# A Perceiver block in one kernel: down-projection chunks loaded into the places of their ternary weights, and an opening split by k-tiles and halves

## The reference

```
x = x + xattn(layernorm(x), ctx)      # q = x Wq', k, v = ctx Wkv'; 16 heads of 64; causal softmax; Wout
x = x + bitmlp(layernorm(x))          # below
x = x + moe(layernorm(x))             # rms norm, top 2 of 8 experts (1024 -> 512 -> 1024) and a shared expert

bitmlp: y = bitlinear(x, w_gate, norm_gate); gate, up = split(y)       # 1024 -> 2 x 2816
        h = silu(gate) * up;  return bitlinear(h, w_down, norm_down)   # 2816 -> 1024
bitlinear(x, w, norm): xn = rms_norm(x) * norm
        xq = round(xn * 127 / max|xn|) * max|xn| / 127                 # one scale per row
        wq = clip(round(w / mean|w|), -1, 1) * mean|w|                 # ternary, one scale per matrix
        return xq @ wq.T
```

## Time and profile before

| | |
|---|---|
| runs, us | 676.99, 677.55, 678.81 |
| profiled execution, us | 677.46 |
| its span, us | 675.9 |
| TensorE busy | 634.3 us, 94% |
| VectorE busy | 490.8 us, 73% |
| ScalarE busy | 411.0 us, 61% |
| GpSimd busy | 145.0 us, 21% |
| moved by DMA | 179.02 MB, mean 265 GB/s |

### The profile page before, as it was taken

One profiled execution on the slowest core, in us unless ns is written; L12 is line 12 of the kernel. 1 busy time (PEld: TensorE's weight loads), 2 busy tenths in 40 slices (PEclk: granted clock), 3 DMA queues, 4 the chain that ended last, 5 costly groups with the idle time before them and its releaser, 6 DMA issues.

```text
span 675.9 us, 9662 instructions
## 1 busy us (share of the span) xinstructions
PE 634.3 (94%) x3275; PEld 476.4 (70%) x3289; DVE 490.8 (73%) x790; ACT 411.0 (61%) x531; POOL 145.0 (21%) x140
## 2 busy tenths in 40 slices
PE   4899999998999999839999999999999999999996
PEld 3778888886885444325467878787878778787875
DVE  5778888879686898688898376729181983654887
ACT  3778888789647998672674275436171771625730
POOL 1363446406000344319500400000000000000042
PEclk9999999999999999959999999999999999999999
DMA  8867776764166878808987639938385697392947
GB/s 340 359 259 291 288 288 234 316 268 176 46 271 269 332 297 362 340 16 305 411 328 263 247 140 380 390 119 332 135 297 198 223 378 330 125 360 69 390 146 277
DMA packets 30969, 179.02 MB, mean 265 GB/s; under 512 B 3808, under 2 KB 3808, under 8 KB 14688
## 3 DMA queue, kind: packets, MB, share of 16 engines
q1 hardware_dynamic: 25920, 161.39, 61.6%
q0 software_dynamic: 5024, 17.30, 6.8%
HBM read 155.62 MB, written 23.07 MB: 264 GB/s over the span
## 4 chain that ended last, share of the span: by engine, by line
PE 56%; DVE 15%; ACT 15%; issue 5%; DMA 5%; POOL 1%; DVEq 1%; SPq 0%; POOLq 0%; ACTq 0%
PE BK L295 12%; PE BK L296 11%; PE BK L301 11%; PE BK L289 9%; ACT PR L1224 4%; ACT RA L1197 3%; PE BK L1700 3%; PE BK L1600 2%; DVE WL L951 2%; PE BK L1823 2%; PE BK L1585 1%; DMA GB<-rows,SLOT 1%; DMA RA<-wbit 1%; DMA rows<-YS 1%; DVE BH L838 1%
## 5 line engine op out<-in xcount | busy, mean ns | idle before, releaser
L295 PE MATMUL BK<-WH,ETH 128*128 128x512 f32 x272 | 107.6, 396 | 1.4 <-ACT ETH L1445 1.3
L296 PE MATMUL BK<-WL,ETH 128*128 128x512 f32 x272 | 106.1, 390 | 0.0
L951 DVE TENSOR_TENSOR WL<-RA,WH 128x2048 fp32r<-128x2048 f32 x40 | 89.4, 2286 | 9.6 <-ACT WH L1412 9.5
L1412 ACT ACTIVATE WH<-RA 128x2048 fp32r<-128x2048 f32 x40 | 73.7, 1922 | 2.3 <-PE BK L1700 2.3
L301 PE MATMUL BK<-WH,ETL 128*128 128x512 f32 x272 | 67.4, 390 | 0.0
L1471 ACT ACTIVATE HTH<-BK 128x256 fp32r<-128x256 f32 x30 | 10.7, 383 | 88.6 <-PE BK L1823 88.5
L295 PEld LDWEIGHTS BK<-WH,ETH 128*128 128x128 f32 x272 | 51.0, 188 | 16.6 <-DVE WL L951 3.8
L649 POOL DMA_INDIRECT GA<-rows,SLOT x4 | 4.9, 1230 | 265.1 <-DVE WL L951 264.1
L301 PEld LDWEIGHTS BK<-WH,ETL 128*128 128x128 f32 x272 | 51.0, 188 | 10.6
L296 PEld LDWEIGHTS BK<-WL,ETH 128*128 128x128 f32 x272 | 51.1, 188 | 10.1
L617 POOL TENSOR_TENSOR HB<-HB,ND (+2 forms) x28 | 31.1, 1128 | 111.4 <-DVE BH L838 110.6
(11 more groups left out here) (260 smaller groups left out, 1409.8 us busy)
## 6 DMA issues: line engine op xcount, KB each, us to landing
RA<-wbit SPq DMA_DIRECT2D x53, 1024.0 KB, 6.4
RA<-wmoe SPq DMA_DIRECT2D x40, 1024.0 KB, 6.7
RC<-wmoe SPq DMA_DIRECT2D x20, 1024.0 KB, 7.5
rows<-ZERO POOLq DMA_DIRECT2D x34, 256.0 KB, 12.4
XG<-rows SPq DMA_DIRECT2D x15, 512.0 KB, 7.2
RD<-wbit SPq DMA_DIRECT2D x7, 1024.0 KB, 5.5
rows<-YS SPq DMA_DIRECT2D x14, 512.0 KB, 6.6
RA<-wqk SPq DMA_DIRECT2D x8, 640.0 KB, 7.4
```

What stands on the lines that cost most here:

```text
L295: e.matmul(dst, sh, mh, start=first and i == 0, stop=False)
L296: e.matmul(dst, sh, ml, start=False, stop=False)
L951: e.tensor_tensor(WL[m][:, q * RAW:q * RAW + RAW], RC[j][:, :], WH[m][:, q * RAW:q * RAW + RAW].bitcast(f32), ALU.subtract)\
L1412: e.activation(WH[m][:, q * RAW:q * RAW + RAW], RC[2 * m + q][:, :], ACT.Copy)\
```

## The change: what it does, and the diff

The opening. The context's two k-tiles are loaded apart, and the value weights' second k-tile comes between the row tiles of x. The value projection is ordered by k-tile and half: for the first k-tile, all four token tiles high by high, then low by high, then high by low, for one half and then the other; then the second k-tile, with the other half first. It uses eight banks. The low part of the second k-tile's weights moves from VectorE to GpSimd. ScalarE takes the root after the first value tile and normalises row tiles 1 and 3. All four row tiles are transposed after the values. The first query and key weights come into RX[1], and ScalarE makes their high part. The key projection goes before the query projection. The first split copies of keys and queries go ahead of sums on ScalarE and VectorE.

The down weights. Chunks 0, 2 and 8 are loaded to where they and their neighbour end (0 and 2 in TD1, 8 in TD2) and rounded and clamped there; 1 and 9 use RD, 3 uses RD2, 4 to 7 RB as before, 10 uses RB[0]. Loads of 0, 1, 2, 3 and 8 wait for no clamp. Three roundings (8, 9, 10) move behind the first two hidden tiles on ScalarE, their clamps behind the second scale on VectorE. The root part of `hidden_scale` becomes `hidden_root`, ahead of the last maxima. The sign of chunk 4 moves behind the last SiLU. The first expert load moves behind the next three.

```diff
-VB = (6, 7, 0, 1)
+VB = ((6, 7, 0, 1), (2, 3, 4, 5))
-DORD = (0, 1, 2, 3, 8, 9, 6, 7, 10)
+DORD = (0, 2, 1, 3, 6, 7, 8, 9, 10)
+RORD = (0, 2, 1, 3, 4, 5, 6, 7, 8, 9, 10)
...
+        RIN = {i: nc.alloc_sbuf_tensor_at(f"RIN{i}", [P, RAW], f32, offset=T.manual_sbuf_range[0] + at)
+               for i, T, at in ((0, TD1, 0), (2, TD1, 8192), (8, TD2, 0))}
+        def down_raw(i):
+            return RIN[i] if i in RIN else {1: RD, 3: RD2, 4: RB[0], 5: RB[1], 6: RB[2], 7: RB[3], 9: RD, 10: RB[0]}[i]
...
         def _(e):
-            e.dma_start(CTX[:, :, :], ctxT).then_inc(s("ctx_in"), 16)
+            e.dma_start(CTX[:, 0, :], ctxT[:, 0, :]).then_inc(s("ctx_in"), 16)
             e.dma_start(RA[0][:, 0:DM], wv[:, 0:DM]).then_inc(s("wv_in"), 16)
-            e.dma_start(RA[0][:, DM:2 * DM], wv[:, DM:2 * DM]).then_inc(in_a[0], 16)
+            e.dma_start(CTX[:, 1, :], ctxT[:, 1, :]).then_inc(s("ctx_in2"), 16)
             for t in range(NT):
+                if t == 2:
+                    e.dma_start(RA[0][:, DM:2 * DM], wv[:, DM:2 * DM]).then_inc(in_a[0], 16)
                 e.dma_start(XRES[:, t, :], x[t * P:t * P + P, :]).then_inc(s(f"x_in{t}"), 16)
+            e.dma_start(RX[1][:, 0:STRIP], wqk[0]).then_inc(in_x[1], 16)
...
-            qk_load(0)
             for n in range(4):
                 sum_load(1 + n, 4 + n, None)
-            for j in range(2):
-                e.dma_start(RX[j][:, :], wbit[8 + j]).then_inc(in_x[j], 16)
+            e.dma_start(RX[0][:, :], wbit[8]).then_inc(in_x[0], 16)
             qk_load(1)
+            e.dma_start(RX[1][:, :], wbit[9]).then_inc(in_x[1], 16)
...
-            down_load(0, 0, None)
+            down_load(1, "raw_d")
...
                 bit_load(n, 8 + n, "tern_a", 1 + n)
+            down_load(0, in_x[0])
             e.wait_ge(s("zq"), NT)
-            down_load(1, 1, None)
+            down_load(2, in_x[1])
+            down_load(3, "raw_e")
+            down_load(8, "raw_8")
             for n in range(4):
                 bit_load(n, 12 + n, "tern", 5 + n)
-            for n in range(2):
+            for n in range(4):
                 bit_load(n, 16 + n, "tern", 9 + n)
-            down_load(2, 0, 1)
-            for n in range(2, 4):
-                bit_load(n, 16 + n, "tern", 9 + n)
-            down_load(3, 1, 2)
...
-            down_load(8, 0, 3)
...
-            down_load(9, 1, 4)
             for n in range(2):
                 bit_load(n, 2 * GC + 4 + n, "tern", 17 + n)
-            down_load(10, 0, 5)
+            e.wait_ge(s("ternd"), DORD.index(1) + 1)
+            down_load(9, "raw_d")
+            bit_load(0, 2 * GC + 10, "tern_a", 5)
...
-                for j in range(6):
+                for j in (1, 2, 3, 0, 4, 5) if first else range(6):
...
+            for n, q in enumerate((1, 0)):
+                cs = slice(q * 512, q * 512 + 512)
+                e.wait_ge(s("wv_hi"), n + 3)
+                e.wait_ge(s("wv_lo"), 2)
+                e.tensor_tensor(WVL[:, 1, cs], RA[0][:, DM + q * 512:DM + q * 512 + 512], WVH[:, 1, cs].bitcast(f32),
+                                ALU.subtract).then_inc((s("wv_lp"), free_a[0])[n], 1)
+            for q, at in enumerate((slice(0, WQA * P), slice(WQA * P, STRIP))):
+                if q == 0:
+                    e.wait_ge(s("xn"), 2)
+                e.wait_ge(s("wq_hi"), q + 1)
...
+                e.tensor_tensor(lo, RX[1][:, at], hi.bitcast(f32), ALU.subtract).then_inc((s("wq_a"), free_a[0])[q], 1)
...
             absum(2, slice(5, 6), 16)
+            k_split(0)
             absum(4, slice(7, 8), 16)
-            k_split(0)
+            q_split(0)
             absum_x(1, 9)
-            q_split(0)
...
-            down_clamp(9, RD16)
+            down_clamp(3)
             last_block(2)
             last_maximum(0)
             last_maximum(1)
             last_block(3)
+            hidden_root(0, 2)
             last_maximum(2)
             last_maximum(3)
             hidden_scale(0, 2)
...
-            down_clamp(6, RB16[2])
-            down_clamp(7, RB16[3])
-            down_clamp(10, RD16A)
+            down_clamp(6)
+            down_clamp(7)
+            hidden_root(2, 2)
             for n in range(4, 8):
                 last_maximum(n)
             hidden_scale(2, 2)
+            down_clamp(8)
+            down_clamp(9)
+            down_clamp(10)
             hidden_integers(2)
...
-            for n in range(4):
+            v_evac(0)
+            root(e, col(2), col(3))
+            for n in range(1, 4):
                 v_evac(n)
-            root(e, col(2), col(3))
+            row_norm(1)
             v_evac(4)
             v_evac(5)
+            row_norm(3)
             xt_evac(0)
             xt_evac(1)
             v_evac(6)
+            xt_evac(2)
             v_evac(7)
-            xt_evac(2)
             xt_evac(3)
...
+            k_split(0)
             absum(1, slice(4, 5), 16)
             absum(3, slice(6, 7), 16)
+            q_split(0)
             e.wait_ge(in_x[0], 16)
             e.activation(RX[0][:, :], RX[0][:, :], ACT.Abs, accum_out=ACCW[:, 8:9]).then_inc(sum_x[0], 1)
-            k_split(0)
-            q_split(0)
...
             group(3)
-            rounded_down(RD[:, :], s("raw_d"), 1)
             group(4)
-            rounded_down(RD2[:, :], s("raw_e"), 1)
+            rounded_down(0)
             group(5)
-            rounded_down(RD[:, :], s("raw_d"), 2)
             group(6)
-            rounded_down(RD2[:, :], s("raw_e"), 2)
+            rounded_down(2)
             group(7)
-            rounded_down(RD[:, :], s("raw_d"), 3)
             gate_block(8, 0)
             gate_block(8, 1)
-            rounded_down(RD2[:, :], s("raw_e"), 3)
+            rounded_down(1)
             gate_block(8, 2)
             gate_block(8, 3)
-            rounded_down(RB[0][:, :], in_b[0], 6)
+            rounded_down(3)
             for n, (c, t) in enumerate(TAIL):
...
-                if n == 1:
-                    rounded_down(RB[1][:, :], in_b[1], 6)
-                elif n == 3:
-                    sign_down(4, 0, 7)
-                elif n == 4:
-                    rounded_down(RB[2][:, :], in_b[2], 5)
-                elif n == 6:
-                    rounded_down(RB[3][:, :], in_b[3], 5)
+                if n in (1, 3, 4, 5):
+                    rounded_down({1: 4, 3: 5, 4: 6, 5: 7}[n])
+            sign_down(4, 0, 5)
...
             hidden_t(0)
-            rounded_down(RD[:, :], s("raw_d"), 4)
-            sign_down(5, 1, 8)
+            sign_down(5, 1, 6)
             hidden_t(1)
+            rounded_down(8)
+            rounded_down(9)
+            rounded_down(10)
             hidden_t(2)
...
+            def values_first(q):
+                cs = slice(q * 512, q * 512 + 512)
+                for n, (A, B) in enumerate(((CTH, WVH), (CTL, WVH), (CTH, WVL))):
+                    e.wait_ge(*((s("wv_hi"), q + 1), (s("ct_lo"), 1), (s("wv_lo"), q + 1))[n])
+                    for t in range(NT):
+                        e.matmul(bank[VB[q][t]], A[:, 0, t * P:t * P + P], B[:, 0, cs], start=n == 0, stop=False)
...
+            values_first(0)
+            values_first(1)
+            e.wait_ge(s("ct_lo"), 2)
+            e.wait_ge(s("wv_lp"), 1)
+            values_rest(1)
+            e.wait_ge(free_a[0], 1)
+            values_rest(0)
             e.wait_ge(s("const"), 15)
-            x_rows(0)
-            x_rows(1)
-            values(6)
-            values(7)
-            x_rows(2)
-            x_rows(3)
-            e.wait_ge(s("v_ev"), 2 * NT)
-            e.wait_ge(s("xt_lo"), 2 * NT)
+            e.wait_ge(s("v_ev"), NT)
+            for t in range(NT):
+                x_rows(t)
+            e.wait_ge(s("v_ev"), 6)
...
             e.wait_ge(s("tern_a"), 6)
-            e.wait_ge(s("ternd"), 8)
+            e.wait_ge(s("ternd"), 6)
             down_group(0, 1)
             down_group(1, 1)
             e.wait_ge(s("ternd"), 9)
```

More of the change, by code:

```diff
@@ L574, in zero_rows, with w_split @@
                 e.dma_start(src.rearrange("a (u v) -> (a u) v", u=2), ZERO[:, :]).then_inc(s("zero"), 16)
-            def w_split(c, first, second=False):
+            def w_split(c, second=False):
                 for q, at in enumerate((slice(0, WQA * P), slice(WQA * P, STRIP))):
                     if q == 0:
-                        e.wait_ge(in_a[0], c * 16 + 32)
-                        if not first and not second:
+                        e.wait_ge(in_a[0], c * 16 + 16)
+                        if not second:
                             e.wait_ge(s("pn"), c * 2 - 2)
-                    if not first:
-                        e.wait_ge(s(("k_pe", "q_pe")[q]), c)
+                    e.wait_ge(s(("wq_pe" if second else "k_pe", "q_pe")[q]), c)
                     hi, lo = (T[:, :, :].rearrange("p a b -> p (a b)")[:, at] for T in (WQH, WQL))
@@ L667, in _, with context_lo @@
-            e.wait_ge(s("ln"), 1)
-            for t in range(NT):
+            def context_lo(m):
```

(56 more changed lines are left out.)

140 lines of the change are left out of this document (66 added, 74 removed).

## The result

The kernel after takes 669.5 us, the median of four runs (669.24 to 670.50); the kernel before took 677.9 beside it (four runs, 676.99 to 678.81). The ratio is 0.9877, with a 95% interval of 0.9855 to 0.9898: 8.4 us faster. The forecast was 664.0, the range 661.0 to 669.0. The sign was right, the gain was over-estimated by 5.5 us, and the measured time lies 0.5 us outside the range. The profiled execution took 670.50 us, 6.96 less than the one of before.

A forecast was written before the change was run, and what follows sets the result against it. TensorE's pace was taken to bound all long stages, with two large waits, at the start and at the hidden rows. 677.46 - 2.3 (opening) - 11.4 (tail) = 663.8, forecast as 664.0 us, range 661.0 to 669.0.

The forecast's parts named there:

- The opening: Start to first exponentials: exponentials at 37.3 instead of 39.6, worth 2.3 us, with bounds of 0.5 to 3.4.
- The tail: Gate products' end to hidden tile 2: tile 2 starts at 308.4 instead of 319.73, a gain of 11.4 us.
- the walk along VectorE's queue: Late gate stage: VectorE's work timed piece by piece, so TensorE transposes at 287.1, 1.5 us after the gate products end.
- a rival of the down stage: Down stage: VectorE becomes the bound, 2 to 6 us late, clamps taking 1.13 instead of 0.68; 666 to 670, chance 0.10.
- May arrive a microsecond late … Nothing.: Gate stage: three down loads in one 7.5 us burst delay a gate load a microsecond; TensorE 6.9 us ahead, no cost.
- The clock in the tail: Rival: after the gate products TensorE's clock falls, losing 2.2 to 3.5 us; 666.0 to 667.3, chance 0.2.
- a row of the kernel before: Opening, 25.4 to 29.2: TensorE did only transposes and its clock stayed at 1.00, so transposes seem to hold it.
- The rule that it weighed against that row: Opening: transposes don't engage the full clock, so it would fall there, costing 2 to 3.5 us; chance 0.05.
- No new wait at hidden tile 2: Down stage: late clamps and VectorE's integers for tile 2 are ready before TensorE needs them, by 0.5 us.
- The sign of chunk 4: Tail: ScalarE runs it after the last SiLU, 286.3 to 288.2, delaying its first copy of transposed rows.
- The slower rival: Down stage: the clock falls and stays low through all 176 down products, 35 us in sum; 699, chance 0.02.

The follow-up runs named there:

- e12: e9 with the opening of the kernel before, so only the down weights' part of the change plus e9's edits; 667.52 us.
- e13: e9 timed again, on the same chip as e12; 666.22 us.
- e1: Kernel after with the loads of down chunks 2, 3 and 8 taken out of their burst and spread behind gate loads; 669.21 us.
- e6: Kernel after with 20 extra matmuls, results unread, filling TensorE's wait ahead of the hidden transposes; 668.2 us.
- e5: Kernel after with down chunk 1's clamp and half the last chunk pair's maxima moved behind tile 0's integers on VectorE; 667.16 us.
- e2: Kernel after with only down chunk 8's load moved out of the burst, behind the gate loads; 669.12 us.
- e3: Kernel before with only the opening's part of the change; 677.09 us.
- e9: Kernel after with the edits of e1 and e5 and 9 of the extra matmuls of e6; 665.9 us.
- e4: Kernel before with only the down weights' part of the change; 669.87 us.
- e8: Kernel after with ten extra matmuls, results unread, among the opening's row-tile transposes; 669.45 us.
- e7: Kernel after with one weight sum of ScalarE and one of VectorE moved from before the exponentials into the first pair; 680.18 us.
- e11: e7 with the third pair's query and key weight load going first on the sync queue; 679.86 us.

## Why the prediction was right and wrong

**By its steps, the sum.** 13.7 us were forecast. The opening is worth 1.5 instead of 2.3 in the two profiles (1.3 in e12 and e13). From the gate products' end to hidden tile 2 the forecast had 308.4 - 285.65 = 22.75 us (34.08 before); it took 311.58 - 284.13 = 27.45. These 4.7 us divide into 2.6 for VectorE's list (the gap of e1, 4.1, less 1.5), 1.3 for the late load (5.4 less 4.1) and 0.7 from the transposes to the second down run (9.09 for 8.4), where the clock is: with it held, e6 took 8.20. The tail gained 6.65 us instead of 11.4. Of the 8.4 us between the medians that leaves 1.8 for the opening, inside what its traces show.

**The step that failed: the walk along VectorE's queue.** "VectorE takes tail blocks 0 and 1 by 276.6, a maximum and a clamp by 278.4, blocks 2 and 3 by 280.9" led to a gap of 1.5 us. Without any late load (e1) it is 4.1. The mechanism was right, the root ahead of the late maxima and nobody waiting for a load; the size was off. Taking the gate products' 1.8 us earlier end in e1 into account, its blocks 0 and 1 should have been done by 274.8 and were by 277.3, 2.5 late, and everything behind them (root 3.1, maxima 0.7, chain 1.2) took what was forecast. So the walk was wrong where it starts: its 276.6 is 1.3 us behind TensorE's second tail product, as if VectorE had nothing left to do ahead of these blocks. The kernel before had shown both the backlog and the price of a pair of gate clamps, in rows that the prediction did not read:

```profile
270.24 2.65 DVE L810 TENSOR_SCALAR TX<-RA 128x2048 bf16<-128x2048 int16 x2
...
275.11 2.27 DVE L843 TENSOR_REDUCE AMAX<-HB 128x4 f32<-128x2048 f32 x1
```

Those maxima (`pair_max(3)`) ended at 277.38, after the 276.6 of the forecast, and in the new order four blocks and a clamp stand between them and the end of blocks 0 and 1, 4.0 us in e1. So an end at 276.6 needed the maxima by 272.6, 13.0 us ahead of the gate products' end. They ended 8.3 us ahead of it before, and 10.4 in e1: 2.6 us short, the whole of the missing gap.

Part of the backlog is the price of the clamps. The pair ahead of these maxima took 2.99 us, where pairs elsewhere take 1.28. Over the whole kernel after, the same instruction ranges from 0.68 to 1.76 us (shortest, median, longest in ns):

```profile
L835 DVE TENSOR_SCALAR TG<-RA x12: 676/688/1760, 182.4 to 260.3; 128x2048 bf16<-128x2048 int16 x12
L835 DVE TENSOR_SCALAR TX<-RA x6: 676/1144/1759, 242.1 to 268.8; 128x2048 bf16<-128x2048 int16 x6
```

The long ones stand beside GpSimd's products with norm_down, three of which run from 265.79 to 269.97, across the pair at 267.53. Two pairs and GpSimd's work at that time:

```profile
254.57 3.01 DVE L835 TENSOR_SCALAR TG<-RA 128x2048 bf16<-128x2048 int16 x2
259.68 1.28 DVE L835 TENSOR_SCALAR TG<-RA 128x2048 bf16<-128x2048 int16 x2
```

```profile
251.62 5.42 POOL L625 TENSOR_TENSOR HB<-HB,ND  x4 [7.45 <-DVE BH L862]
264.56 5.41 POOL L625 TENSOR_TENSOR HB<-HB,ND  x4 [7.52 <-DVE BH L862]
```

All four pairs that run while GpSimd multiplies took 2.36 to 3.01 us, all three that run while it rests 1.28 or 1.29. The Trainium skill (SBUF — State Buffer, Who interferes with whom) says that VectorE and GpSimd share one pair of ports, which a VectorE instruction in a two-port mode also takes (a tensor_scalar such as the clamp can run in one), and that whoever has it blocks the other for a whole instruction; the trace agrees, with a clamp of 0.68 stretched to 1.76. No run here took GpSimd's work away, so that GpSimd is the cause is argued from the rows only. The prediction did name such clamps (1.13 for 0.68), but as a rival of the down stage. They mattered 20 us and more earlier, where VectorE has no idle time. That each piece in its list counts there is shown by e5.

**"May arrive a microsecond late … Nothing."** The load was late by 4.58 us of ScalarE's time, and the slack of one group of products had to carry it through a stretch in which VectorE fills nearly its whole time; 0.9 to 1.3 us of the gap are shown by e1 and e2. Costing the burst against TensorE's need was the error: VectorE was the engine without slack.

**The clock in the tail.** The forecast took it to hold, and gave its fall 0.2 and 2.2 to 3.5 us. It fell in the kernel after and in each execution with an unfilled gap (3.55 us and more), and cost 0.7 to 0.9 us (e6), since the transposes at half speed partly hide behind the integers that they wait for anyway. No run had an unfilled gap of 1.5 us, so whether the clock would have held there, and the fall comes from the failed step, is not shown.

**The opening.** The first matmul (6.29 for 7.0), the first low part (22.32 for 22.3) and the last (27.65 for 27.4) came as forecast or sooner. The scores came at 35.18 for 34.4, the exponentials at 38.13 for 37.3: ScalarE's chain of copy, sum, value copy and table load was right in its parts, but starts with a query copy that ends at 34.4 and not at 33.5. Most of that is the clock, which the prediction held by a row of the kernel before. Where it held, the scores came at 34.1 to 34.7 and the exponentials at 37.0 to 37.6 (e2, e3, e5, e9, e13), as forecast. The rule that it weighed against that row, that the full clock doesn't engage for PE-mode transposes (the Trainium skill, TensorE: Matmul & The Clock Gate, Part 4: PE-mode transpose), is borne out by the kernel after, e1 and e6, and not by five others with the same opening (e2, e3, e5, e9, e13), in which the clock stayed at 1.00 through 20 to 28. With the opening of before it held in the kernel before and e12 and fell in e4 (0.50 from 30 to 32). The fall costs some 0.6 us at the exponentials and at the gate products' end (e8), less than the timed runs can tell. So against the 39.60 of the profile before, the 2.3 us were there at the exponentials in these executions (2.0 to 2.6). That as much reaches the end of the program is shown by no timed run.

**What held.** No new wait at hidden tile 2: VectorE's integers ended at 310.46, 1.1 us ahead of TensorE (a margin of 0.5 was forecast), so the three late roundings and clamps are free. From the second down run to hidden tile 2 it took 12.95 us for 12.9. The sign of chunk 4 ended at 288.03 as forecast, but held nobody, since the integers came later still. The slower rival (clock low through all down products) did not come: the clock was back at 293.9.

## What to carry to other kernels

When a wait is closed, the next bound is the engine that feeds it: walk that engine's list with the durations that its operations have at that place in the trace, not with the shortest one, and start from the last place where it stood idle, not from the first operation of interest. A load's lateness is to be costed against the engine with the least slack between it and the end. Work that is off the path can be moved only if the load that refills its buffer, and all behind it on the queue, can wait too (e7 and e11 lost 10 us by two sums). Idle matmuls in a wait can be worth it, where TensorE's clock would fall just ahead of dense work (0.9 us in e6's trace).

## What the runs showed of the hardware

The same opening, instruction for instruction, ran the stretch 24 to 28 at 0.57 in the kernel after and at 1.00 in e9 and e13, so that one profile does not decide whether the clock holds. With 2.10 us of extra matmuls in a gap of 2.6 us (e9) the clock was 1.00 throughout to 296. And a pair of VectorE's 128x2048 clamps took 1.28 us alone and 2.36 to 3.01 beside GpSimd's products.
